# A four-layer graph network: first norms by halves, layer 1's sums from one product, a one-operation mask, and a last unit in three parts

## The reference

```
L0: adj @ (x @ W0) + b0
L1: res[i,j] = si[i] + sj[j] + adj[i,j]*w_r + g_b,  sj = x @ w_j, si = x @ w_i
    out = (res @ x) @ W1 + b1
L2: x_h = elu(x @ Wi + bi);  e = sigmoid(a_tgt[i] + a_src[j] + be) * mask
    mask = adj where adj != 0, else 0.005
    out = [elu([e @ x_h, x_h * rowsum(e)] @ Wn + bn), x_h] @ Wm + bm
L3: 5 gated steps:  m = adj @ h;  z = sigmoid(W3 m + U3 h + ..)
    r = sigmoid(W4 m + U3 h + ..);  c = tanh(W5 m + U5 (r*h) + ..);  h = (1-z) h + z c
```

## Time and profile before

| what | value |
|---|---|
| runs | 1234.6, 1237.77, 1240.07 us |
| profiled execution | 1235.95 us, of which the span from first to last instruction is 1234.0 us |
| TensorE busy | 1172.3 us (95%) |
| VectorE busy | 927.5 us (75%) |
| ScalarE busy | 684.7 us (55%) |
| DMA | 93.66 MB, mean 76 GB/s |
| mean granted clock of TensorE | 0.988 of full |

### The profile page before, as it was taken

The page is one execution under the profiler, slowest core; times in us unless marked ns, Lnnn a source line. Parts: engine busy times, 40 slices in busy tenths (PEclk is TensorE's granted clock), DMA queues, the critical chain, the costliest instruction groups (busy, mean ns, idle before and its releaser), DMA issues.

```text
span 1234.0 us, 15530 instructions
## 1 busy us (share of the span) xinstructions
PE 1172.3 (95%) x5232; PEld 907.4 (74%) x5232; DVE 927.5 (75%) x2071; ACT 684.7 (55%) x1119; POOL 74.5 (6%) x80
## 2 busy tenths in 40 slices
PE   7979899799999999999999999999999999999995
PEld 5866368577777878877777677887777768788884
DVE  5987986588878886677887886685798788554656
ACT  4336762666566675356567565546457657544443
POOL 0110010000000011001000001000001002000001
PEclk9999999899999999999999999999999999999997
DMA  7222330132222322121232322211332322000001
GB/s 249 87 76 94 102 112 1 34 120 78 94 94 85 95 86 88 41 77 60 92 96 78 128 94 69 69 52 52 104 111 86 111 78 86 18 1 1 1 1 35
DMA packets 92575, 93.66 MB, mean 76 GB/s; under 512 B 9104, under 2 KB 62992, under 8 KB 92496
## 3 DMA queue, kind: packets, MB, share of 16 engines
q1 hardware_dynamic: 92352, 92.27, 23.0%
q0 software_dynamic: 144, 0.40, 0.1%
HBM read 65.35 MB, written 27.29 MB: 75 GB/s over the span
## 4 chain that ended last, share of the span: by engine, by line
PE 58%; DVE 22%; ACT 6%; issue 4%; DMA 4%; SPq 4%; POOL 2%; DVEq 0%; POOLq 0%; ACTq 0%
PE ps L813 33%; PE ps L818 4%; PE ps L820 4%; PE ps L819 4%; PE ps L936 4%; DVE ring L1544 3%; PE ps L831 3%; ACT x L1133 3%; DMA mk<-mask_scratch 2%; SPq L693 2%; DVE tl L1359 2%; DVE hT L1598 1%; DVE v L1595 1%; PE ps L824 1%; DVE ml L1359 1%
## 5 line engine op out<-in xcount | busy, mean ns | idle before, releaser
L813 PE MATMUL ps<-adj_hi,xh 128*128 128x512 f32 x672 | 281.6, 419 | 13.1 <-DVE xl L1359 7.1
L813 PE MATMUL ps<-adj_hi,xl 128*128 128x512 f32 x672 | 263.0, 391 | 0.0
L813 PE MATMUL ps<-adj_lo,xh 128*128 128x512 f32 x672 | 262.5, 391 | 0.0
L813 PEld LDWEIGHTS ps<-adj_hi,xh 128*128 128x128 f32 x672 | 126.7, 189 | 50.4 <-issue 19.0
L813 PEld LDWEIGHTS ps<-adj_lo,xh 128*128 128x128 f32 x672 | 126.8, 189 | 32.6 <-issue 8.9
L813 PEld LDWEIGHTS ps<-adj_hi,xl 128*128 128x128 f32 x672 | 126.4, 188 | 27.3
L1577 DVE TENSOR_TENSOR r<-r,hT 128x512 f32<-128x512 f32 x80 | 53.7, 688 | 76.8 <-ACT r L1271 76.8
L818 PE MATMUL ps<-mh,wh 128*128 128x512 f32 x240 | 101.9, 425 | 6.7 <-DVE ml L1359 5.2
L1544 DVE TENSOR_TENSOR ring<-ring,mk 128x512 f32<-128x512 f32 x128 | 86.9, 685 | 27.2 <-ACT ring L1206 23.9
L1206 ACT ACTIVATE ring<-fh,asn 128x512 f32<-128x512 f32 x96 | 67.3, 719 | 62.6 <-DVE mk L1359 21.5
L1128 ACT ACTIVATE mh<-ps 128x512 fp32r<-128x512 f32 x80 | 47.2, 590 | 92.0 <-PE ps L813 92.0
(11 more groups left out here) (295 smaller groups left out, 2374.2 us busy)
## 6 DMA issues: line engine op xcount, KB each, us to landing
mk<-mask_scratch SPq DMA_DIRECT2D x128, 256.0 KB, 2.8
state_scratch<-v SPq DMA_DIRECT2D x60, 256.0 KB, 2.0
tl<-state_scratch SPq DMA_DIRECT2D x192, 64.0 KB, 2.0
x<-in_x SPq DMA_DIRECT2D x8, 512.0 KB, 4.1
out<-x SPq DMA_DIRECT2D x7, 512.0 KB, 3.2
layer_scratch<-fk SPq DMA_DIRECT2D x12, 256.0 KB, 2.3
fr<-layer_scratch SPq DMA_DIRECT2D x48, 64.0 KB, 2.0
fh<-target_scratch SPq DMA_DIRECT2D x12, 256.0 KB, 3.3
```

The costliest lines, as they stand in the source:

```text
L813: mm = pe.matmul(dst, a[:, t, :], b[:, t, cut(h)], start=(t == 0 and i == 0), stop=(t == T - 1 and i == 2))
```

## The change

- Batches 0 and 1 (`HALVED`): the norms of layers 0, 1 and 2 are done by halves of four tiles (`v0a`, `v0b`, `n0a`, `n0b` and so on), the rests too (`l1a`, `l1b`), and layer 1's product with adj waits for its second half at the fifth tile. `start_natural` of these two batches becomes the pieces `n2a`, `n2b` (ScalarE) and `l2a`, `l2b` (VectorE).
- Layer 1's sums: x gets a column of ones, and `sums` multiplies x transposed by [x, 1], 129 columns where it was 2. VectorE takes sum sj x from it with w_j, so the row products with w_j go. k is added as the bias of ScalarE's copy of the product with adj, which is also scaled by w_r. So the scaled W1, the second product of `rows` and the buffer `kb` go.
- Mask: ScalarE scales the tile by 1/0.005, and VectorE makes (x == 0) + x in one operation. Two weights of layer 2 are scaled by 0.005 on ScalarE to make up for it.
- The last unit: parts of 512, 256 and 256 columns, each with its own banks. W4 is kept beside W4 - W3: the reset gates of parts 1 and 2 have a bank apart from their update gates and use W4; that of part 0 still adds W4 - W3 in the update gate's bank, after the sigmoid has read it.
- The lists of all engines are in another order, in `first` and in most of the units 0 to 29. SP's loads and its code are otherwise as they were.

The core of the diff (the calls of `ending` are written here without their lambdas):

```
-first m0a:0 m0b:0 m0a:1 y0a:0 y0b:0 m0b:1 y0a:1 y0b:1 m0a:2 m0b:2 m1a:0 m1b:0 sums:0 m1a:1 rows:0 y1a:0
-first m1b:1 y1b:0 sums:1 y0a:2 y0b:2 rows:1 y1a:1 y1b:1 t2a:0 t2b:0 pja:0 pjb:0 tha:0 thb:0 tga:0 tgb:0
-first m1a:2 e00:0 ...
+first m0a:0 m0b:0 y0a:0 y0b:0 m0a:1 m0b:1 y0a:1 sums:0 m1a:0 m1b:0 y0b:1 m0a:2 rows:0 y1a:0 sums:1 y1b:0
+first m1a:1 m1b:1 t2a:0 m0b:2 rows:1 t2b:0 pja:0 pjb:0 y1a:1 y1b:1 y0a:2 y0b:2 tha:0 thb:0 tga:0 tgb:0 t2a:1
+first e00:0 e01:0 e02:0 t2b:1 e03:0 pja:1 e04:0 e05:0 e06:0 sums:2 m1a:2 ...
     "ACT":
-first x0:0 x0:1 x0:2 m0a:0 weights:0 m0b:0 m0a:1 m0b:1 n0:0 ...
+first x0:0 x0:1 x0:2 m0a:0 weights:0 m0b:0 mask:0 mask:1 mask:2 mask:3 mask:4 mask:5 n0a:0 m0a:1 n0b:0
+first ... n1a:1 s00:0 s01:0 s02:0 n1b:1 t2a:1 s03:0 s04:0 s05:0 t2b:1 s06:0 n0:2
     "DVE":
-first x0:0 x0:1 weights:0 c0:1 c0:0 mask:0 x0:2 y0a:0 y0b:0 mask:1 v0:0 ...
+first x0:0 c0:0 weights:0 y0a:0 x0:1 v0a:0 y0b:0 c0:1 v0b:0 mask:0 x0:2 l1a:0 mask:1 l1b:0 ...
+first ... rows:0 l1b:1 y1a:0 sums:1 v1a:0 y1b:0 d1:1 v1b:0 rows:1 c2:0 pja:0 pjb:0 y1a:1 y0a:2 v1a:1 y1b:1
+first as:0 v1b:1 y0b:2 s00:0 s01:0 s02:0 v0:2 s03:0 s04:0 s05:0 s06:0 c2:1 l1:2 s07:0 ...
@@ sums, TensorE
-                        mm = pe.matmul(ps[:, bank, 0:2], x[:, t, :], f["sv"][:, t, 0:2],
+                        mm = pe.matmul(ps[:, bank, 0:D + 1], x[:, t, :], x_wide(b)[:, t, :],
@@ mask, VectorE
-                dve.tensor_scalar(noedge, stage[t], 0.0, ALPHA, ALU.is_equal, ALU.mult)
-                dve.tensor_tensor(stage[t], stage[t], noedge, ALU.add)
+                dve.scalar_tensor_tensor(out=stage[t], in0=stage[t], scalar=0.0, in1=stage[t],
+                                         op0=ALU.is_equal, op1=ALU.add)
@@ last unit: columns, banks of product, update gate, reset gate, candidate
+        LAST = ((slice(0, HALF), 2, 4, 4, 6), (slice(HALF, HALF + QUARTER), 3, 5, 0, 7),
+                (slice(HALF + QUARTER, N), 2, 1, 4, 3))
@@ ending, TensorE
+                product(0)
+                candidate(*prev, halves=(0,)); candidate(*prev, halves=(1,))
+                of_state(0, Z_BANK)
+                of_state(1, Z_BANK)
+                product(1, {2: update(0), 4: of_state(1, R_BANK), 6: reset(0), 7: of_state(2, Z_BANK)})
+                product(2, {1: turn_state(prev, 0), 2: turn_state(prev, 1), 3: reset(1), 4: update(1),
+                            6: begin_candidate(0), 7: end_candidate(0)})
+                of_state(2, R_BANK); begin_candidate(1); end_candidate(1)
+                reset(2); update(2); begin_candidate(2); turn(0)
+                end_candidate(2); turn(1); turn(2)
@@ ending, ScalarE
+                split(0); candidate(*prev); update(0); reset(0); split(1); round_reset(0); reset(1)
+                update(1); round_reset(1); last_candidate(0); split(2); last_candidate(1); reset(2)
+                update(2); round_reset(2); last_candidate(2); output_apply(B - 2); output_apply(B - 1)
@@ ending, VectorE
+                split(0); update(*prev); last_reset(0); state_lo(prev, 0); last_reset_lo(0); split(1)
+                state_lo(prev, 1); last_keep(0); last_reset(1); last_reset_lo(1); last_keep(1)
+                output_stats(B - 2); split(2); last_update(0); last_reset(2); last_update(1)
+                last_reset_lo(2); last_keep(2); output_moments(B - 2); last_update(2); last_sum(0)
+                output_stats(B - 1); output_moments(B - 1); last_sum(1); (statistics of two tiles)
+                last_sum(2); (statistics of two tiles); output_moments(B); output_apply(B)
```

More of the change, by code:

```diff
@@ L91 @@
[L91 to L94, removed]
+first m0a:0 m0b:0 y0a:0 y0b:0 m0a:1 m0b:1 y0a:1 sums:0 m1a:0 m1b:0 y0b:1 m0a:2 rows:0 y1a:0 sums:1 y1b:0
+first m1a:1 m1b:1 t2a:0 m0b:2 rows:1 t2b:0 pja:0 pjb:0 y1a:1 y1b:1 y0a:2 y0b:2 tha:0 thb:0 tga:0 tgb:0 t2a:1
+first e00:0 e01:0 e02:0 t2b:1 e03:0 pja:1 e04:0 e05:0 e06:0 sums:2 m1a:2 pjb:1 e07:0 m1b:2 e10:0 e11:0 e12:0
@@ new lines @@
+first rsa:0 e13:0 e14:0 tha:1 e15:0 rows:2 rva:0 e16:0 e17:0 thb:1 y1a:2 y1b:2 tga:1 tgb:1 y2a:0 rsb:0 e00:1
+first e01:1 e02:1 rvb:0 e03:1 e04:1 e05:1 m0a:3 e06:1 e07:1 y2b:0 m0b:3 e10:1 e11:1 e12:1 y0a:3
+unit0 @2 e13:1 e14:1 e15:1 y0b:3 e16:1 e17:1 @4 rsa:1 @7 rsb:1 @8 pja:2 rva:1 sums:3 m1a:3 rvb:1 m1b:3 y2a:1 rows:3 y1a:3 y2b:1 pjb:2 y1b:3 @19 th0:2 th1:2 @22 th2:2
+unit1 @22 e00:2 e01:2 e02:2
+unit2 @12 e03:2 @21 e04:2 e05:2 @22 e06:2 @26 rsa:2
+unit3 @2 e07:2 @3 rva:2 @8 e10:2 @9 y2a:2 e11:2 @22 e12:2 e13:2 @24 e14:2
@@ L95 @@
+unit4 @2 e15:2 @4 rsb:2 @10 e16:2 @17 e17:2 @18 rvb:2 @22 y2b:2
+unit5 @13 pja:3 pjb:3 @21 th0:3 th1:3 @23 th2:3
+unit6 @22 e00:3 e01:3 e02:3
+unit7 @18 e03:3 e04:3 @21 e05:3
+unit8 @1 rsa:3 @9 e06:3 e07:3 @10 rva:3 @18 y2a:3 e10:3 e11:3 @21 e12:3
+unit9 @4 e13:3 @16 e14:3 e15:3 @18 e16:3 @21 rsb:3 e17:3
+unit10 @4 rvb:3 @19 y2b:3 m0a:4 @23 m0b:4 @25 y0a:4 @27 y0b:4
+unit11 @19 sums:4 @21 m1a:4 @23 m1b:4
 unit12 @15 rows:4 @21 y1a:4 @22 y1b:4
-unit13 @19 m0a:5 @22 m0b:5 pja:4 y0a:5 pjb:4 @23 y0b:5 @26 th0:4 th1:4
@@ L97 @@
-unit14 @3 th2:4 @11 m1a:5 @18 m1b:5 e00:4 sums:5 e01:4 e02:4 e03:4 @21 e04:4 e05:4 rows:5 @22 e06:4
-unit15 @8 e07:4 y1a:5 rsa:4 @12 e10:4 e11:4 e12:4 rva:4 @22 y1b:5 e13:4
-unit16 @2 e14:4 y2a:4 e15:4 e16:4 @10 e17:4 rsb:4 @15 rvb:4 @22 y2b:4
+unit13 @21 m0a:5 @23 m0b:5 pja:4 pjb:4 y0a:5 @25 y0b:5 @27 th0:4 th1:4
+unit14 @10 th2:4 sums:5 @18 m1a:5 @21 m1b:5 e00:4 e01:4 @24 rows:5 e02:4
+unit15 @11 e03:4 @16 e04:4 e05:4 y1a:5 e06:4 rsa:4 e07:4 y1b:5 @22 e10:4 @25 e11:4 e12:4
+unit16 @1 e13:4 e14:4 e15:4 rva:4 @6 e16:4 @7 e17:4 @9 y2a:4 @11 rsb:4 @16 rvb:4 @22 y2b:4
@@ L106 @@
[L106 to L110, removed]
+unit21 @1 y0a:6 @6 y0b:6 @22 sums:6 m1a:6
+unit22 @9 m1b:6 @11 rows:6 @18 y1a:6 @21 y1b:6
+unit23 @19 m0a:7 @22 m0b:7 pja:6 y0a:7 pjb:6 @23 y0b:7 @26 th0:6 th1:6
@@ new lines @@
+first mask:3 v0a:1 sums:0 d1:0 mask:4 mask:5 mask:6 mask:7 y0b:1 v0b:1 l1a:1 rows:0 l1b:1 y1a:0 sums:1 v1a:0
+first y1b:0 d1:1 v1b:0 rows:1 c2:0 pja:0 pjb:0 y1a:1 y0a:2 v1a:1 y1b:1 as:0 v1b:1 y0b:2 s00:0 s01:0 s02:0
+first v0:2 s03:0 s04:0 s05:0 s06:0 c2:1 l1:2 s07:0 sums:2 pja:1 d1:2 pjb:1 s10:0 s11:0 s12:0 s13:0 s14:0
+first s15:0 rsa:0 s16:0 s17:0 rows:2 as:1 rva:0 y1a:2 y1b:2 v1:2 y2a:0 s00:1 s01:1 s02:1 v2a:0 rsb:0 s03:1
+first s04:1 s05:1 x0:3 rvb:0 c0:3 s06:1 s07:1 s10:1 y2b:0 s11:1 v2b:0 l2a:0 s12:1 l2b:0 t2a:2 s13:1 s14:1
@@ new lines @@
+first s15:1 s16:1 s17:1 y0a:3 y0b:3 t2b:2 v0:3 rsa:1 rsb:1 l1:3
+unit0 @2 sums:3 rva:1 d1:3 c2:2 pja:2 rvb:1 y2a:1 rows:3 v2a:1 y2b:1 y1a:3 v2b:1 y1b:3 pjb:2 l2a:1 v1:3 @4 l2b:1 th0:2 th1:2 @9 th2:2 @13 ax:2
+unit1 @4 s00:2 s01:2 q00:2 s02:2 q01:2 q02:2 @6 s03:2 @7 s04:2 s05:2
+unit2 @1 q03:2 @4 s06:2 q04:2 q05:2 q06:2 @7 s07:2 s10:2 s11:2 @10 q07:2 @11 rsa:2 @15 q10:2 rva:2 q11:2 s12:2
+unit3 @3 y2a:2 @4 s13:2 s14:2 q12:2 q13:2 @6 q14:2 @7 s15:2 s16:2 q15:2 @11 s17:2 @15 rsb:2 q16:2
+unit4 @4 q17:2 rvb:2 @7 y2b:2 v2:2 t2a:3 @11 t2b:3
```

581 lines of the change are left out of this document (359 added, 222 removed).

## The result

The changed kernel takes 1242.63 us (median of 11 runs, 1240.46 to 1245.08); the kernel before, run beside it, 1237.77. The ratio is 1.0042, with an interval of 1.0028 to 1.0055: slower, where the forecast was 1230.5 and faster. The profiled execution took 1241.95, with a span of 1240.1; the forecast for it was 1228.65.

What follows compares the result with a forecast made beforehand. TensorE bounds the kernel, except where VectorE's chain does early on. Front -4.8, TensorE's work -0.9, units 0, last unit -1.6 sum to -7.3: 1228.65 us profiled, 1230.5 median, range 1220 to 1246 (own range 1226 to 1235).

Steps and rivals of the forecast that it cites:

- point 6: TensorE's own work: sums 0.08 us more per batch, rows 0.2 less, together 0.9 us less.
- point 7: Units 1 to 29: another order with the same work, taken as zero, bounds -4 and +4 us.
- rival D: Units' new order costs 4 us, a piece standing ahead of a gate: 1234.5 us, chance 8%.
- 1, the start: TensorE's start: m0a:1 waits behind y0a:0 and y0b:0, a loss of 8.7 us.
- 2, 80 to 115 us: TensorE waits for VectorE's list before the first attention tile, then for m1a:2: 1.4 us lost.
- 3, 138 to 160 us: m0a:3 and m0b:3 between batch 1's tiles make TensorE the bound there: 6.4 us won.
- rival A: Late start not caught up, VectorE bounds 85 to 175 us, hole before unit 1 stays: 1244.4 us, chance 24%.
- 4, into unit 1: The wait for batch 1's xl before unit 1 goes, with half clock behind it: 7.5 us won.
- 5, small waits: Waits for kb and the second constant row at 48, 66 and 78 us go: 1.0 us won.
- 8, the last unit: Last unit in three parts, 256-column matmuls at 0.12 us: 1.6 us won, bounds +7 and -4.
- rival C: Last unit's 256-column matmuls cost 0.227 us, +7 instead of -1.6: 1239.1 us, chance 8%.
- rival B: VectorE's shorter work cuts point 2's (80 to 115 us) waits, 7.7 us more won: 1222.8 us, chance 20%.

Runs made afterwards that it cites:

- the shift: The changed kernel's wider x buffers put xh and later operands 128 bytes higher; the kernel before with only that shift: 1246.12 us, ratio 1.0086.
- mended addresses: Changed kernel with 992 unused floats between the x buffers and xh, so xh lies 4096 bytes above its place in the kernel before: 1233.81 us, ratio 0.9986.
- 512 bytes: Kernel before with 512 unused bytes ahead of xh, the adjacency buffers staying in place: 1236.81 us, ratio 0.9999.
- all buffers shifted: Kernel before with 128 bytes ahead of the adjacency buffers, so every buffer lies 128 bytes higher: 1234.82 us, ratio 0.998.

## Why the prediction was wrong, point by point

**The step that failed** is point 6, TensorE's own work, and point 7, which has "another order with the same work" and takes zero, with bounds of -4 and +4. The work is the same in number and shape and not in price: an adjacency matmul takes 0.2325 us instead of 0.2277, and from unit 1 to the last unit the changed kernel takes 975.8 us instead of 966.1, 9.7 more and outside the bounds. The diff showed the wider buffers (`D + 1`); I had counted their extra columns and the products that read them, not the place of all buffers behind them. No row of the trace before could have given the price, but the edit stood there to be named as an unknown. Without the shift the time would be 0.9986 x 1237.77 = 1236.0 there, just above the forecast's own range of 1226 to 1235. Of the order alone, point 7's zero is uncertain, within its bounds. With mended addresses this stretch takes 965.0 us in one trace and 967.0 to 970.0 in eight others; with the old order 966.1, 967.1 (512 bytes) and 970.9 (all buffers shifted, the execution of 1239.07 us). TensorE's idle gaps between 240 and 1190 us add up to 16.0 to 19.6 us in the new order and to 13.7 to 16.6 in the old one. So the order probably costs some 2 us there; neither the zero nor rival D's 4 is shown.

**1, the start**: right. m0a:1 starts at 30.15 (forecast 30.65), y0b:0 at 28.39 (29.0), after a wait of 4.23:

```profile
23.04 1.13 PE L865 MATMUL ps<-wf,fm 128*128 128x128 f32 x8
28.39 2.05 PE L865 MATMUL ps<-wf,fm 128*128 128x128 f32 x8 [4.23 <-ACT fm L1238]
30.15 0.80 PE L847 MATMUL ps<-adj_hi,xh 128*128 128x512 f32 x1
```

That is 8.4 us later than before (21.75), where the forecast had 8.9. The half clock behind the hole took 1.7 us in this trace (0.10 of 10.15 and 0.25 of 2.85 us in the stretches above), where the forecast had 1.9. What the late start costs in the end is less than 8.7: putting it right gave 3.1.

**2, 80 to 115 us**: about right. VectorE waits 10.11 us for `rows:1`, then needs 14.9 to the first tile (forecast 15), which it takes up at 98.65 (99.5), and m1a:2 starts at 113.04 (115). The forecast's 1.9 for the clock was too little here: the granted clock of 0.91 and 0.92 over 40 us is 3.4 us. It had taken too little for the time before as well (2.3, where 0.83 over 20 us is 3.4). The rows of VectorE:

```profile
83.73 2.16 DVE L1633 SCALAR_TENSOR_TENSOR x<-ps,sva,x 128x128 f32<-128x128 f32 x8 [10.11 <-PE ps L923]
98.65 1.30 DVE L1695 TENSOR_TENSOR ring<-ring,mk 128x512 f32<-128x512 f32 x2 [0.54 <-ACT ring L1329]
111.76 1.23 DVE L1510 TENSOR_TENSOR tl<-x,th 128x1024 fp32r<-128x1024 f32 x1 [0.47 <-ACT th L1238]
```

**3, 138 to 160 us**: wrong, the 6.4 us were not won. I said that m0a:3 and m0b:3 stand between the tiles and make TensorE the bound. They stand behind the sixth and the eighth; the hole is ahead of the first. There VectorE goes through `rows:2`, a row of products, sums and v1:2, 10.7 us from 135.50 to 146.24, and TensorE waits:

```profile
147.07 4.51 PE L980 MATMUL ps<-ring,fm 128*128 128x512 f32 x6 [2.05 <-DVE ring L1695]
152.08 1.10 PE L997 MATMUL ps<-fh,wx 128*128 128x512 f32 x2 [0.49 <-DVE fr L1689]
157.41 0.47 PE L847 MATMUL ps<-adj_hi,th 128*128 128x512 f32 x1 [0.80 <-DVE tl L1510]
```

Two runs that moved work there (m0a:3 ahead, v1:2 behind) got the wait back within 25 us. Half of rival A was right: TensorE waits for tiles of batch 1 between 140 and 175 us, and VectorE's last tile of that batch starts at 182.16, which is A's sign. It was wrong in its second half, since the hole before unit 1 did not stay.

**4, into unit 1**: right in kind, late in size. The wait for `xl` is gone. But the second half norm's rounding ends at 222.7 (forecast 214.6) and the rest behind it at 224.9 (217.3), so most of the room that the forecast saw is used up, and unit 1 starts at 228.42 (224). The front as a whole was to give 4.8 and gave 2.4 (228.42 for 230.8), which is less than the 6.4 of point 3 would take away, so the other points together won more than I had summed. Most of that is the start, which costs 3.1 where the sum has 8.7.

**5, small waits**: right in kind. TensorE's idle time between 50 and 80 us went from 0.7 us to none.

**6, sums and rows**: `sums` 2.02 us for 16 records against 1.84: 0.18 a batch where I took 0.08, within the bounds.

**8, the last unit**: right, and in its detail. Matmuls of 256 columns come every 0.12 us, so rival C is out. So is the prediction's reading of the Trainium skill (TensorE: Matmul & The Clock Gate, The mechanism), by which the load isn't hidden; the estimate from it was 0.214:

```profile
1214.97 0.28 PE L847 MATMUL ps<-adj_hi,xl 128*128 128x256 f32 x1
1215.09 0.28 PE L847 MATMUL ps<-adj_hi,xh 128*128 128x256 f32 x1
1215.21 0.28 PE L847 MATMUL ps<-adj_lo,xh 128*128 128x256 f32 x1
1215.33 0.28 PE L847 MATMUL ps<-adj_hi,xl 128*128 128x256 f32 x1
```

The passes of part 1 wait for VectorE's split (0.57), and VectorE's backlog eats the rest of the lead: the last transposes start 26.1 us after the last unit's first product, 28.6 before, but the last sum comes only 3 us behind them, where it took 1.1:

```profile
1219.88 0.39 PE L852 MATMUL ps<-mh,wh 128*128 128x256 f32 x1 [0.57 <-DVE ml L1510]
...
1230.37 0.66 PE L1153 MATMUL ps<-ident,hT 128*128 128x128 f32 x2 [1.43 <-DVE hT L1851]
...
1233.33 0.41 DVE L1857 TENSOR_TENSOR x<-ps,x 128x256 f32<-128x256 f32 x1
...
1236.20 1.12 DVE L1898 TENSOR_SCALAR x<-x,mvo,rso 128x128 f32<-128x128 f32 x4 [1.12 <-POOL rso L812]
```

That is 1.2 us for the forecast's 1.6, but the kernel before's 37.1 was itself long: the two halves took 36.5 and 36.3 in the runs with 512 bytes and with all buffers shifted, and 36.5 in the new order, where the three parts took 35.7 to 35.8. So 0.6 to 0.8 is what they are worth, half of the forecast.

**The sum again.** Forecast -7.3. Without the shift -1.7 in the medians (interval -2.7 to -0.6) and -5.0 between the two profiled executions; the one with mended addresses was the second fastest of its twelve runs, so the medians count. In that trace the 5.0 are 2.4 up to unit 1, 1.1 up to the last unit and 1.4 in it; in the other traces of this order the stretch between takes 2 to 5 us more, which is what the medians miss of the 5.0. The pace brings the median from -1.7 to +4.9. Of rival B's 7.7 us about 2.7 are to be had by the ratios, 1.3 by the traces, in the run with `rows:1` early.
